# First feed-forward of a four-layer kernel: the copy of a tile's first expert rows on another engine, and a new order of four steps

## The reference

```
q = x @ w_q;  k = x @ w_k                       # per head
gates = sigmoid(x @ w_gate)                     # token, head, expert
gm    = one_hot(argmax(gates)) * gates          # one expert per token and head
values = einsum('bhne,ehdk,bnd->bhnk', gm, value_experts, x)
attn   = softmax(causal(q @ k.T * 64**-0.5))
out    = einsum('bhij,bhjk->bhik', attn, values)
out    = einsum('bhne,ehkd,bhnk->bhnd', gm, output_experts, out).sum over heads
x      = x + tanh(g_ffn[0]) * out
```

## Time and profile before

| | |
|---|---|
| median of 3 runs | 2107.25 us |
| the profiled execution, its own time | 2104.33 us |
| its span, first to last instruction | 2102.2 us |
| TensorE busy | 1916.6 us, 91% |
| VectorE busy | 1537.1 us, 73% |
| ScalarE busy | 836.1 us, 40% |
| GpSimd busy | 721.2 us, 34% |
| mean granted TensorE clock | 0.950 |

### The profile page before, as it was taken

How to read it: one execution, slowest core, us unless ns; L and a number is a source line. 1 busy time by engine, 2 the same in 40 slices (tenths; PEclk the granted TensorE clock), 3 DMA queues, 4 the chain that set the end, 5 groups by cost and what they waited for, 6 DMA issues and landing times. The chain is left out here.

```text
span 2102.2 us, 41789 instructions
## 1 busy us (share of the span) xinstructions
PE 1916.6 (91%) x14339; PEld 1025.3 (49%) x14339; DVE 1537.1 (73%) x3177; ACT 836.1 (40%) x1500; POOL 721.2 (34%) x953
## 2 busy tenths in 40 slices
PE   5869999998998988999999999979998999989975
PEld 3734444444444444555555554435663444436641
DVE  4767877877877776777777776857785666768978
ACT  6622112112012005666666663315652223225655
POOL 2541111102112105677676774455730000013222
PEclk9569999999999999999999999989998999999985
DMA  5403203212132041000000000000002524221001
GB/s 140 149 1 82 63 21 79 45 39 61 35 66 61 20 113 76 2 2 1 0 0 0 0 2 1 1 8 15 15 7 80 129 73 118 63 64 20 16 1 40
DMA packets 60080, 89.74 MB, mean 43 GB/s; under 512 B 23720, under 2 KB 42024, under 8 KB 55472
## 3 DMA queue, kind: packets, MB, share of 16 engines
q1 hardware_dynamic: 59952, 88.10, 17.1%
HBM read 80.91 MB, written 2.97 MB: 40 GB/s over the span
## 5 line engine op out<-in xcount | busy, mean ns | idle before, releaser
L955 POOL TENSOR_TENSOR l0f_v<-l0f_val,l0f_top 64x256 f32<-64x256 f32 x128 | 78.2, 611 | 484.2 <-DVE l0f_val L1233 476.7
L1062 PE MATMUL l0f_acc<-l0f_z,w_all 128*128 128x512 f32 x512 | 228.5, 608 | 15.0 <-DVE l0f_z L1271 15.0
L1011 PE MATMUL l0f_work<-w_all,l0f_xs 128*128 128x512 f32 x384 | 183.4, 600 | 15.0 <-DVE l0f_val L1228 14.2
L1062 PEld LDWEIGHTS l0f_acc<-l0f_z,w_all 128*128 128x128 f32 x512 | 99.0, 195 | 143.9 <-issue 123.1
L255 POOL TENSOR_SCALAR var_eps<-mean_var 128x4 f32<-128x4 f32 (+1 forms) x64 | 16.8, 263 | 375.8 <-DVE mean_var L239 373.6
L1477 PE MATMUL l1x_proj_v<-l1x_wvo,l1x_cs 128*64 128x512 f32 x512 | 139.2, 622 | 0.0
L1233 DVE COPY_PREDICATED l0f_val<-l0f_oh,l0f_work 128x512 f32<-128x512 int32 x160 | 116.7, 729 | 22.8 <-PE l0f_work L1011 7.9
L2881 ACT ACTIVATE l2f_act_g<-l2f_pg 128x512 f32<-128x512 f32 x104 | 61.6, 594 | 146.3 <-PE l2f_pu L2816 134.3
L2824 PE MATMUL l2f_acc<-l2f_hid,w_all 128*128 128x512 f32 x208 | 107.4, 598 | 10.2 <-DVE l2f_hid L2962 10.2
L2956 DVE TENSOR_TENSOR l2f_hu<-l2f_act_g,l2f_pu 128x512 f32<-128x512 f32 x104 | 71.1, 684 | 60.3 <-ACT l2f_act_g L2881 58.8
L1011 PEld LDWEIGHTS l0f_work<-w_all,l0f_xs 128*128 128x128 f32 x384 | 66.1, 190 | 87.8 <-issue 32.2
(11 more groups left out here) (400 smaller groups left out, 4375.2 us busy)
## 6 DMA issues: line engine op xcount, KB each, us to landing
l0f_first_mask<-onehots SPq DMA_DIRECT2D x32, 512.0 KB, 5.8
w_all<-onehots SPq DMA_DIRECT2D x32, 512.0 KB, 11.8
w_all<-combination SPq DMA_DIRECT2D x40, 256.0 KB, 5.1
w_all<-in_weights SPq DMA_DIRECT2D x1, 4640.0 KB, 16.8
l0x_m_b<-running_max SPq DMA_DIRECT2D x16, 256.0 KB, 4.3
w_all<-combination SPq DMA_DIRECT2D x16, 224.0 KB, 4.3
w_all<-combination SPq DMA_DIRECT2D x16, 192.0 KB, 4.1
w_all<-combination SPq DMA_DIRECT2D x16, 160.0 KB, 4.1
```

The costliest lines, as they stand in the source:

```text
L955: nc.gpsimd.tensor_tensor(v2[a * SEQ:(a + 1) * SEQ, t % 2, b, :, :], val[r, t % 2, :, :].rearrange("p (c a) k -> p c a k", a=2)[:, :, a, : ...
L1011: nc.tensor.matmul(value_banks[e % 3][:, :], xs[:, t * P:(t + 1) * P], ve[:, e, :], start=True, stop=True).then_inc(ve_done, 1)
L1062: nc.tensor.matmul(acc[:, :], oe[:, n % E, n // E, :], z[:, n % Z, :], start=(n == 0), stop=(n == C * E - 1)).then_inc(acc_done, 1)
```

## The change

The copy of the first expert's rows goes from VectorE to ScalarE (`copy_first`), with a semaphore of its own; `pick_done` then counts seven picks per tile (`PICKS`). On ScalarE, the copy for tile t + 1 stands ahead of the copy of the turned probabilities of tile t; the exponential of a group's tile 0 moves from the end of the group before to behind the first such copy. The sum of the probabilities stands behind the pick of expert 3, the scaling behind that of expert 4, and their turn on TensorE behind the eighth product. `pick_experts` is split: the last step, which waits for the tanh, is now `gate_halves` and stands behind the masked outputs.

```diff
+        first_copied = sem("first_copied")
+        PICKS = E - 1
...
-                    pool.wait_ge(pick_done, count((n + 1) * E))
+                    pool.wait_ge(pick_done, count((n + 1) * PICKS))
...
-                            after(pe, pick_done, u * G * E)
+                            after(pe, pick_done, u * G * PICKS)
...
                 def expert_values(g, t, between=None, later=None):
                     for e in range(E):
                         n = (g * G + t) * E + e
+                        if e == 0 and t == 0:
+                            pe.wait_ge(qk_copied, count((g + 1) * 2 * C))
                         if e == 2 and t == 0:
                             pe.wait_ge(y_ready, count(g))
-                        after(pe, pick_done, n - 1 if e < 2 else n - 2)
+                        if e == 3:
+                            pe.wait_ge(first_copied, count(g * G + t + 1))
+                        else:
+                            after(pe, pick_done, (g * G + t) * PICKS + (-1, 0, -2, 0, 1, 2, 3, 4)[e])
...
-                        if e == 5 and later:
+                        if e == E - 1 and later:
                             later()
...
-                    pe.wait_ge(pick_done, count((g + 1) * G * E))
+                    pe.wait_ge(pick_done, count((g + 1) * G * PICKS))
...
+                def copy_first(g, t):
+                    n = g * G + t
+                    act.wait_ge(ve_done, count(n * E + 1))
+                    after(act, v2_ready, (n - 1) * 4)
+                    nc.scalar.activation(val[:, t % 2, :, :], value_banks[0][:, :].rearrange("p (h k) -> p h k", h=H),
+                                         ACT.Copy).then_inc(first_copied, 1)
+
...
                 def group(g, more, normed=True):
                     for t in range(G - 1):
+                        copy_first(g, t + 1)
+                        if t == 0:
+                            exp(g, 0)
                         copy_pT(g, t)
                         exp(g, t + 1)
                         copy_oT(g, t)
...
                     if more:
-                        exp(g + 1, 0)
+                        copy_first(g + 1, 0)
 
                 copy_q(0, range(C))
                 copy_k(0, range(C))
                 gate_tanh(0)
+                copy_first(0, 0)
                 edge_scalar(core, nc, act, edge, misc)
-                exp(0, 0)
...
+                    return ch
+
+                def gate_halves(u, ch):
                     dve.wait_ge(tanh_done, count(u + 1))
-
                     ch.link(nc.vector.tensor_scalar(top[:, 2, :], top[:, 1, :], 0.5, 0.5, ALU.mult, ALU.add))
                     ch.done()
 
                 def pick(g, t, between=()):
-                    for e in range(E):
-                        n = (g * G + t) * E + e
-                        dve.wait_ge(ve_done, count(n + 1))
+                    n = g * G + t
+                    for e in range(1, E):
+                        dve.wait_ge(ve_done, count(n * E + e + 1))
                         w3 = value_banks[e % 3][:, :].rearrange("p (h k) -> p h k", h=H)
-                        if e == 0:
-                            after(dve, v2_ready, (g * G + t - 1) * 4)
-                            nc.vector.tensor_copy(val[:, t % 2, :, :], w3).then_inc(pick_done, 1)
+                        if e == 1:
+                            dve.wait_ge(first_copied, count(n + 1))
                         else:
-                            dve.wait_ge(pick_done, count(n))
-                            dve.sem_inc(may_pick, 1)
-                            m_e = bcast(oh[:, t * H:(t + 1) * H, e], 2, HD).bitcast(I32)
-                            nc.vector.copy_predicated(val[:, t % 2, :, :], m_e, w3).then_inc(pick_done, 1)
-                        if 0 < e <= len(between):
-                            between[e - 1]()
+                            dve.wait_ge(pick_done, count(n * PICKS + e - 1))
+                        dve.sem_inc(may_pick, 1)
+                        m_e = bcast(oh[:, t * H:(t + 1) * H, e], 2, HD).bitcast(I32)
+                        nc.vector.copy_predicated(val[:, t % 2, :, :], m_e, w3).then_inc(pick_done, 1)
+                        if between and e in (3, 4):
+                            between[e - 3]()
...
                     if more:
-                        pick_experts(g + 1)
+                        ch = pick_experts(g + 1)
                     masked_outputs(g)
                     if more:
+                        gate_halves(g + 1, ch)
                         pick(g + 1, 0)
...
-                pick_experts(0)
+                gate_halves(0, pick_experts(0))
```

## The result

The changed kernel took 2094.6 us, the median of 6 runs (2090.8 to 2097.0), beside 2111.2 us for the kernel before on the same chip; the ratio is 0.9923, with a 95% interval of 0.9908 to 0.9939. The profiled execution took 2090.8 us, span 2088.7, against 2104.3 and 2102.2. The forecast was 2083 with a range of 2072 to 2096. Its sum for the profiled executions was -23.5 us; they differ by -13.5.

A forecast was written before the change was run, and what follows sets the result against it. TensorE was busy for 91% of the span; VectorE paced the tiles, and a tanh wait halted TensorE. Tiles -3.5, halt -14.6 and clock -5.4 summed to -23.5 us, 2080.8 profiled; forecast 2083 us, range 2072 to 2096.

The forecast's parts named there:

- all up to the end of group 0: Group 0: its tiles forecast slower by +1.1 us, its output products earlier by -2.0 us.
- Part 1: Tiles: expert 0's copy leaves VectorE for ScalarE; -0.69 us a loop group, -3.5 us for tiles in all.
- P1: Start of a tile's pick of expert 1 on VectorE; forecast 2.94 or 2.46 us after the previous tile's S.
- S: Start of a tile's subtraction on VectorE, the mark from which the forecast counts its times.
- rival A: Tiles: ScalarE is never late with the copy, 8 us more gain, 2075 us; chance 0.12.
- this stretch keeps its length: VectorE from P1 to S in a tile: same work before and after, 7.80 to 7.82 us.
- Part 2: Order inside a tile: banks freed sooner, TensorE waits about 0.8 us instead of 1.54 + 0.68; later turn costs nothing.
- This hides and costs nothing: End of a tile: ScalarE's output copy starts at S + 1.26, 1.3 us after the values, so their delay is hidden.
- rival D: Tiles: turn behind all products delays values and copies at 24 places, so slower, 2125 us at 3 us late; chance 0.06.
- Part 3: Group end: tanh step behind the masked products, output products start 2.10 us earlier, 2.0 in group 0; -14.6 us in all.
- Rival C: Group end: masked products find another wait, so Parts 3 and 4 give nothing, 2104 us; chance 0.07.
- Part 4: First output products of three long loop groups: low TensorE clock goes with the halt; -5.4 us, bounds 0 and -5.4, or +4.

The follow-up runs named there:

- e3: The changed kernel with ScalarE's copy for tiles 2 and 3 one place earlier, right behind the exponential; ratio 0.9901, groups of 78.24 us.
- e7: The changed kernel with pick_done counting eight a tile as before, instead of seven; ratio 0.9925, groups of 78.46 us.
- e1: The kernel before with only the step behind the tanh moved behind the masked outputs; ratio 0.9917, median 2092.2 us.
- e4: The changed kernel with the old order in a tile: sum and scaling behind experts 1 and 2, turn behind product 5; ratio 0.9918, groups of 78.83 us.
- e9: e3 with the old order inside the tile, by e4's edit; ratio 0.9896, groups of 77.85 us.
- e2: The changed kernel with the step behind the tanh back ahead of the masked outputs; ratio 1.0024 to the kernel before.
- e0: The changed kernel unaltered, measured and profiled a second time; ratio 0.9922, loop groups 473.8 us in sum.
- e6: e3 with the next tile's scores and the turn of the probabilities between the seventh and eighth product on TensorE; ratio 0.9896, groups of 77.89 us.
- e8: e6 with e7's counter, pick_done counting eight; ratio 0.9852, median 2076.3 us, groups of 77.3 us.
- e5: The changed kernel with the first rows copied by VectorE again, new order and moved tanh step kept; ratio 0.9936, groups of 79.83 us.

## Why the prediction was right, and where it was not

The time came into the range, but only 1.4 us below its upper end, and the half of the change that carries the gain was the one named. Of the sum, 10 us are missing. Term by term, from the profiled executions:

| term | forecast | measured |
|---|---|---|
| tiles of six loop groups | -4.1 | -1.1 |
| halt before the output products, six groups | -12.6 | -11.3 |
| clock in the loop | -5.4 | -5.4 |
| all up to the end of group 0 | -0.9 | 0.0 |
| last group | -0.5 | +0.5 |
| rest of the kernel | 0 | +3.9 |

**Part 1.** The queue on ScalarE was right: P1 at S + 2.94 forecast, 2.97 and 2.96 measured, the copy at S + 2.22, and e3 shows that it is this order that holds it; rival A, the copy never late, is out. The step that failed is "this stretch keeps its length". It grew from 7.80 to 7.90 us in each tile. From the start of the last loop group to S of its last tile it went from 33.62 (638.23 to 671.85) to 33.44 us (624.13 to 657.57), -0.18 where the forecast had -0.69. e7, which changes only what the thresholds are counted in, has 7.79 or 7.80 from P1 to S again and 33.01 us up to S of the last tile (622.79 to 655.80): -0.61. So 0.43 of the missing 0.51 us is the price of the counter in sevens, a part of the change that the sum had at nothing. Of the rest, 0.1 is the first pick of tile 1 (S + 0.71 instead of 0.62), which stays in e7. In the unrolled groups, where a threshold is a constant, P1 to S was 7.70 before and after.

In group 0, P1 to P1 went as worked out (S + 2.94 and 2.46), but I had guessed the old P1 of tile 3 instead of reading it: it was at S + 1.94, which makes the step 0.5, not 0.3. Tile 1 came 0.37 us later for a reason that I did not find, and 0.2 came from ahead of the tiles. Together 0.8 of the 0.9 us.

**Part 2.** "This hides and costs nothing" was right for the output copy, whose 1.3 us of slack was never used up, so rival D did not come. It missed the other follower of the values: logits and query products. They began at S + 0.94 instead of S + 0.74, and the group's end moved by 0.2 us with them. e1, e4 and the changed kernel show it: 45.23, 45.30 and 45.53 us from S of tile 3 to the end. The experiments show more: the new order is no gain. With the copy on ScalarE it costs 0.14 us a group (e4 to the changed kernel), and with the early copy 0.39 (e9 to e3, 77.85 to 78.24).

**Part 3.** In place of 2.10 us the halt gave 1.89, which is 2.1 less those 0.2. What was named as late next, TensorE's last projections, is what the trace has. e1 alone gave 2.2. Rival C is out.

**Part 4.** The low clock left the loop, as forecast. Over all kernels without the halt it fell in one of sixty loop groups; with the halt in five of twelve (the kernel before and e2). The Trainium skill, "TensorE: Matmul & The Clock Gate", section "Why this matters for your kernels", would have had it stay, since it ties it to longer idle gaps; the runs disagree. But what decides it stays open: seven of the twelve halts of 1.94 us were not followed by a low clock, and the one fall in e9 came behind two halts of 0.98 and 0.81 us that stand in the two groups before it as well, without one.

**The rest.** I had written that all behind the stage shifts as it is. The work does; its clock does not. Over the twelve profiled executions the rest took 1309 to 1310 us in three, 1313 to 1314 in three, and 1316 to 1317 in six. e0 against its twin shows a step of 3.4 us between two executions of one program. e6 and e8, which hold the change, have 1309.7 and 1309.1, as the kernel before has 1309.2. So 3.9 of the 10 us is no effect of the change.

The last group is 0.45 us shorter up to S of its last tile (33.13 to 32.68), as forecast; it is unrolled, so the counter costs nothing there. From that S to its end it is 0.97 us longer (38.90 to 39.87), and the clock is lower: 0.65 instead of 0.78 on average up to the output products. e0 has the same (39.83), so this may well come from the change; the forecast had looked for low clocks in the loop groups alone.

The medians differ by 16.6 us and the profiles by 13.5, because the profiled execution lay 6.9 us below the median of its kernel before and 3.8 below it after. The forecast took 24.2 us off the median of 2107.25. Of the 11.6 us by which 2083 missed 2094.6, 7.7 are the gain that was forecast too large, and 3.9 come from the kernel before, whose median was 2111.2 when more runs were taken. That the time still lies in the range is luck in part.

**What the copy is worth.** The Trainium skill, "TensorEngine Tiling (Array Packing)", section "PSUM Bottleneck", advises to share the emptying of the banks between both engines. Here it took 2.6 us of VectorE's busy time out of a group (63.1 in e1, 60.5 in e4), but never as much out of its length. In the new order the group became 0.86 us shorter (e5 to the changed kernel). In the old order e4 is no shorter than e1, but it pays for the counter in sevens as well; with the 0.5 us of e7 taken off, the copy would be worth about 0.5 us there, an estimate. Where the copy stands in ScalarE's order counts as much: one place earlier gave 0.73 us in the new order (the changed kernel to e3) and 0.98 in the old one (e4 to e9, 78.83 to 77.85).

## What to carry to other kernels

What it pays to take work off the engine that sets the pace depends on where it lands in the other engine's queue: list what is ahead of it there, and place it before whatever nobody waits for. A short step that waits for a slow answer should stand behind the work that doesn't need it; that single move gave as much here as the whole change. When a change alters what a semaphore counts, look at the waits in hardware loops too, and compare only kernels that count alike: e1 against e4 seemed to say that the copy is worth nothing, and differed in the counter as well.

## What the runs showed of the hardware

- In the hardware loop the same instructions stood further apart with other thresholds in their waits. With thresholds of seven times the tile number beside eight times for the other counter, picks stood 0.875 us apart; with eight for both, 0.86; with constants in unrolled code also 0.86. It came to 0.5 us a group of 28 picks (e7), and 0.57 in e8 against e6. Whether the factor seven itself or the second product per wait costs it was not tried.
- TensorE's clock fell to the lower level (1.2 GHz) behind a halt of 1.94 us in five loop groups of twelve that are alike (the kernel before and e2), and once behind two halts of 0.98 and 0.81 us, which in the two groups before were not followed by it. What decides it is not shown.
- The same program's identical stretches behind the stage took 1313.1 and 1316.5 us in two executions, with mean clocks of 0.96 and 0.95.
